# A cross-attention block with a routed feed-forward layer: ScalarE issues the transfer of the maxima rows

## The chip, the core and the metric

The kernel runs on one core of a Trainium2 chip. The metric is the device time of one execution in microseconds. Five engines run their own programs in order and meet only at semaphores: PE (TensorE), DVE (VectorE), ACT (ScalarE), POOL (GpSimd) and SP (SyncE, which here only issues transfers). Transfers run on 16 DMA engines, whoever issues them.

## What is computed

The input is 32 batches of 128 tokens of width 128, with a context of the same shape. Cut to what matters:

```
q, k, v = layernorm(x) @ Wq + bq, ctx @ Wk + bk, ctx @ Wv + bv        # 16 heads of width 8
s   = q k^T / sqrt(8)                                                  # 128 x 128 per head and batch
x1  = x + tanh(g0) * (softmax(s) v) @ Wout + ...
y   = layernorm(x1);  expert = argmax(y @ Wg)                          # 8 experts, 512 places each
out = x1 + tanh(g1) * gate * (relu(y @ W1[e] + b1[e]) @ W2[e] + b2[e])
```

A softmax needs the largest score of each row subtracted before the exponential. This kernel subtracts it inside a second matrix product: the negated maximum, split into two bf16 parts, stands in two more rows of the packed q operand, against rows of ones in the packed k operand.

## The kernel before, in words

**Tiles and stages.** The 32 batches are worked in 8 groups of four. A schedule of steps numbered `c` runs through all engines; step `c` belongs to group `g = c // 4` at place `j = c % 4`, and each engine does in step `c` the work of several batches at different ages: scores of batch `c` (`scores`, L476, in four quarters q of four heads), maxima of batch `c` on DVE (`top`, L735), the transposition of the maxima of batch `c-1` on PE (L537) and their eviction to `mrow` on ACT (L649), the shifted scores of batch `c-2` (`shifted`, L491, four quarters) and their exponentials on ACT (`exps`, L624), the products with the values of batch `c-3` (L505), and normalisation and output projection of batches `c-4` and `c-5`. The steps 8 to 23 run in a hardware loop; the others are written out.

**Packing.** q and k are kept as three bf16 parts each, and the matrix products run over the stacked parts. `pack` (L327) moves the parts of a whole group from `parts_k` and `parts_q` into `kp` and `qp`: six transfers of 128 KB for k and six for q. SP issues those of group g+1 in step `j == 2` of group g. It first waits until shifted scores of two groups back have been read (`p_T`, from group 2 on) and for `k_split`, later for `q_split`, which POOL (L258) or, at the start, DVE signals. Group g+1 can start its scores (L476) when all twelve have landed.

**The rows of maxima.** The 8 KB of `mrow` go into rows 48 and 49 of `qp` by one transfer a batch (L342), issued by SP in step `n+1` after it has waited for ACT's eviction (`a_m`). In step `j == 2` it stands between the six transfers of k and the six of q. PE waits for it (`m_in`) before the first quarter of the shifted scores of that batch, in step `n+2`.

**What orders the work.** SP's program is in order: whatever stands behind a wait for `a_m` is issued after it. In each step ACT evicts `mrow` between the exponentials of quarter 0 and those of quarter 1, and `shifted` uses two PSUM banks in turn, so that its quarter q waits for the exponentials of quarter q-2 (`a_exp`). After step 39 come eight experts of the feed-forward layer, which the change does not touch.

Of the kernel before, what the change touches and what calls it, by code (L numbers as in the profile page):

```python
# [27 lines left out]
GB = 4  # L28
# [7 lines left out]
def flamingo_kernel(nc, x, ctx_in, g_xattn, g_ffn, w_qkv, b_qkv, w_out, b_out, wg, w1, b1, w2, b2, consts, out):  # L36
    B, L, D = x.shape
# [10 lines left out]
    KR = SLOTS * HD  # L48
    KM = KR + 2
# [7 lines left out]
    with ExitStack() as ctx:  # L57
        def sb(name, shape, dt=F32):
            return ctx.enter_context(nc.sbuf_tensor(name, shape, dt))
# [4 lines left out]
        def sem(name):  # L64
            return ctx.enter_context(nc.semaphore(name))

        def sem2(name):
            return [sem(name + "0"), sem(name + "1")]
# [47 lines left out]
        qp = [sb(f"qp{i}", [P, HEADS, GT], BF16) for i in range(2)]  # L116
# [6 lines left out]
        mrow = [sb(f"mrow{i}", [2 * HEADS, P], BF16) for i in range(2)]  # L123
# [46 lines left out]
        c_in, q_in, k_in, m_in = sem2("c_in"), sem2("q_in"), sem2("k_in"), sem2("m_in")  # L170
# [7 lines left out]
        a_cT, a_xT, a_q, a_k, a_m = sem("a_cT"), sem("a_xT"), sem("a_q"), sem("a_k"), sem("a_m")  # L178
# [23 lines left out]
        def per_batch(v, r, per=1):  # L202

            return v if r is None else r * (per * BODY) + v

        def per_group(v, r, per=1):
            return v if r is None else r * (per * BODY // GB) + v

        def is_batch(n):
            return 0 <= n < B  # L210

        def is_group(g):
            return 0 <= g < NG
# [60 lines left out]
        def _(sp):  # L274
# [13 lines left out]
            def load_w1(e, at):  # L288

                sp.dma_start(w1s[e % 2][:], moved(w1[e % 2], at)).then_inc(w1_in[e % 2], 16)  # L290
# [6 lines left out]
            def ready(*values):  # L297

                for v in values:
                    if not isinstance(v, int):  # L300
                        sp.reg_mov(scratch, v)
# [27 lines left out]
            def step(c, r):  # L329
                j, g = c % GB, c // GB  # L330
                if j == 2 and is_group(g + 1):
                    pack(g + 1, r, 0, SLOTS)
                loads, stores = j == 0 and is_group(g + 2), j == 0 and is_group(g - 2)
                if j == 0:
                    ready(per_batch(c, r), per_group(g + 1, r), per_batch(GB * (g - 2) + GB, r))
                if is_batch(c - 1):
                    sp.wait_ge(a_m, per_batch(c, r))
                if is_batch(c - 1):
                    n, p = c - 1, (c - 1) % 2
                    G = n // GB  # L340
                    t0 = (n % GB) * L
                    sp.dma_start(qp[G % 2][KR:KM, :, t0:t0 + L], mrow[p][:]).then_inc(m_in[p], 16)  # L342
                if stores:
                    sp.wait_ge(v_x1, per_batch(GB * (g - 2) + GB, r))
                    sl = bass.ds(per_group((g - 2) * GB, r, GB), GB)
                    sp.dma_start(out_v[:, sl, :], rec[g % 2][:, :, D:2 * D]).then_inc(x1_out, 16)
                if loads:
                    if g + 2 >= 2:
                        sp.wait_ge(p_cT, per_group(g + 1, r))
                    sp.dma_start(c_sb[g % 2][:], ctx_v[:, bass.ds(per_group((g + 2) * GB, r, GB), GB), :]).then_inc(c_in[g % 2], 16)  # L350
                if j == 2 and is_group(g + 1):
                    pack(g + 1, r, SLOTS, 2 * SLOTS)
                if c == -8:
                    late_loads()
                if c == -7:
                    sp.dma_start(x_sb[:, 2 * GB:, :], x_v[:, 2 * GB:, :]).then_inc(x_in[2], 16)
                if c == -1:
                    sp.wait_ge(v_ones, 1)
                    for i in range(2):
                        sp.dma_start(kp[i][KR:KM, :, :], ones_row[:]).then_inc(s_ones, 16)  # L360
                if c == B + 2:
                    for e in range(2):
                        load_w1(e, None)
                        load_w2(e, None)
                    sp.dma_start(b1_all[:], b1.rearrange("e (f p) -> p e f", p=P),
                                 allow_slow_non_contiguous=True).then_inc(b12_in, 16)
                    sp.dma_start(b2_all[:], b2.rearrange("(a e) n -> a (e n)", a=1).broadcast_to([P, E * D])).then_inc(b12_in, 16)

            run_steps(step, sp)

            def load_xe(e, at):
# [45 lines left out]
        def _(pe):  # L417
# [48 lines left out]
            def scores(n, q, r):  # L466

                G, t0 = n // GB, (n % GB) * L
                if q == 0 and n % GB == 0:
                    pe.wait_ge(q_in[G % 2], per_group(96 * (G // 2) + 96, r, 48))  # L470
                    pe.wait_ge(k_in[G % 2], per_group(96 * (G // 2) + 96, r, 48))
                if 4 * n + q >= 2:
                    pe.wait_ge(v_red, per_batch(4 * n + q - 1, r, 4))
                for h in range(4 * q, 4 * q + 4):
                    o = (h % 4) * L
                    mm = nc.tensor.matmul(S[:, q % 2, o:o + L], qp[G % 2][0:KR, h, t0:t0 + L],  # L476
                                          kp[G % 2][0:KR, h, t0:t0 + L], start=True, stop=True)
                mm.then_inc(p_S, 1)
# [123 lines left out]
        def _(act):  # L602
# [23 lines left out]
            def step(c, r):  # L626
                j, g = c % GB, c // GB
                if is_batch(c - 4):
                    n = c - 4
                    act.wait_ge(p_O, per_batch(n + 1, r))  # L630
                    if n >= 2:
                        act.wait_ge(p_back, per_batch(n - 1, r))
                    nc.scalar.activation(oraw[n % 2][:], O[:, n % 2, :], ACT.Copy).then_inc(a_O, 1)
                if is_batch(c - 2):
                    exps(c - 2, 0, r)
                if j == 2 and is_group(g + 2):
                    H = g + 2
                    act.wait_ge(p_cT, per_group(H + 1, r))
                    if H >= 2:
                        act.wait_ge(p_v, per_group(H - 1, r))  # L640
                    nc.scalar.activation(cT[H % 2][:], X[:, 1, :], ACT.Copy).then_inc(a_cT, 1)
                if j == (3 if g + 2 else 2) and is_group(g + 2):
                    proj(1, g + 2, r)
                if is_batch(c - 1):
                    n = c - 1
                    act.wait_ge(p_m, per_batch(n + 1, r))
                    if n >= 2:
                        act.wait_ge(m_in[n % 2], per_batch(16 * (n // 2), r, 8))
                    nc.scalar.activation(mrow[n % 2][:], X[:, 0, 0:P // 2].bitcast(BF16)[0:2 * HEADS, :],  # L649
                                         ACT.Copy).then_inc(a_m, 1)  # L650
                if is_batch(c - 2):
                    exps(c - 2, 1, r)
                if j == (3 if g + 2 else 2) and is_group(g + 2):
                    first_part(1, g + 2, r)
                if is_batch(c - 2):
                    exps(c - 2, 2, r)
                if j == 2 and is_group(g + 2):
                    H = g + 2
                    act.wait_ge(p_xT, per_group(H + 1, r))
                    if H >= 1:  # L660
                        act.wait_ge(p_q, per_group(H, r))
                    nc.scalar.activation(xnT[:], X[:, 0, :], ACT.Copy).then_inc(a_xT, 1)
                if j == 3 and is_group(g + 2):
                    proj(0, g + 2, r)
                if is_batch(c - 2):
                    exps(c - 2, 3, r)
                if j == 1 and is_group(g - 2):
                    G = g - 2
                    act.wait_ge(p_nT, per_group(G + 1, r))
                    nc.scalar.activation(xn2T[:], X[:, 0, :], ACT.Copy).then_inc(a_nT, 1)  # L670
                if is_batch(c - 4):
                    n = c - 4
                    act.wait_ge(p_oT, per_batch(n + 1, r))
                    if n >= 2:
                        act.wait_ge(p_at, per_batch(n - 1, r))
                    nc.scalar.activation(onT[n % 2][:], X[:, 1, 0:L], ACT.Copy).then_inc(a_oT, 1)  # L676
                if j == 3 and is_group(g + 2):
                    first_part(0, g + 2, r)
                if j == 2 and is_group(g - 2):
                    G = g - 2  # L680
                    act.wait_ge(v_ldif, per_group(G + 1, r))
                    nc.scalar.activation(lexp[:], ldif[:], ACT.Exp).then_inc(a_lexp, 1)
# [448 lines left out]
```

## Time and profile before

| | |
|---|---|
| time, median of 3 runs | 491.91 us (491.57 to 496.6) |
| span of the profiled execution | 506.3 us |
| mean granted TensorE clock in it | 0.639 of full speed |
| PE busy | 393.1 us (78%) |
| ACT busy | 157.3 us (31%) |
| DVE busy | 233.6 us (46%) |
| POOL busy | 173.4 us (34%) |
| packets of the hardware queue q1, share of 16 engines | 31.4% |

The page gives no other time for the profiled execution than its span, which is 14.4 us above the median of the runs. The attention stage takes the first 400 us of the span. In the rows below, "L327" is a line of the kernel before, SPq, POOLq and ACTq are the instructions with which an engine issues transfers, and `[1.42 <-DMA qp<-mrow]` means that the engine was idle for 1.42 us before the instruction until that transfer landed.

### The profile page before, as it was taken

Reading aid. Unit: us, or ns where it says so; the run is one execution under the profiler, and the core shown is the slowest. Engines: PE = TensorE matmul, PEld = TensorE weight load, DVE = VectorE, ACT = ScalarE, POOL = GpSimd, SP = SyncE. Lnnn points to the kernel's source line nnn. Section 1 sums busy time; section 2 is a strip of 40 time slices with the busy share of each in tenths; the row PEclk is TensorE's granted clock in tenths of the full one; section 3 lists DMA queues with packets and bytes.
Section 4 is the critical chain, followed back from the end, with each engine's and each line's share of the span. In section 5 each row is a group of like instructions: output and inputs, shape, how many; then the busy total and the mean of one; then the engine's idle time right before and its main releaser. Section 6 shows DMA issues by size and latency. Waiting matters only on the chain.

```text
span 506.3 us, 8841 instructions
## 1 busy us (share of the span) xinstructions
PE 393.1 (78%) x3024; PEld 257.7 (51%) x3024; DVE 233.6 (46%) x710; ACT 157.3 (31%) x322; POOL 173.4 (34%) x200
## 2 busy tenths in 40 slices
PE   2437399999987959998796998479999525999950
PEld 0215256646654745665474565347665322676650
DVE  3609235726734863673586257245441311425440
ACT  1221143433433533333353345123333101313200
POOL 4535131322406522540642281041032260155463
PEclk9975555555557765555776559555555555999995
DMA  6863640521253254225315513530016014356320
GB/s 171 214 137 74 150 78 22 116 55 43 37 63 72 56 62 55 84 35 61 71 51 61 57 65 44 63 64 23 3 38 152 21 54 110 97 157 195 95 75 20
DMA packets 47748, 39.22 MB, mean 77 GB/s; under 512 B 8774, under 2 KB 43291, under 8 KB 47716
## 3 DMA queue, kind: packets, MB, share of 16 engines
q1 hardware_dynamic: 44004, 28.73, 31.4%
q0 software_dynamic: 3712, 10.07, 5.9%
q8 instruction: 19, 0.31, 0.3%
q14 instruction: 13, 0.11, 0.1%
HBM read 13.72 MB, written 12.65 MB: 52 GB/s over the span
## 4 chain that ended last, share of the span: by engine, by line
PE 54%; DMA 23%; SPq 7%; issue 4%; DVE 4%; POOL 3%; another core or an unknown queue 2%; ACT 1%; POOLq 0%; DVEq 0%; ACTq 0%
DMA qp<-parts_q 15%; PE O L505 9%; PE S L476 9%; PE TS L491 8%; SPq L327 6%; DMA qp<-mrow 5%; PE X L532 5%; PE X L578 4%; PE X L442 3%; PE X L527 3%; PE TS L568 2%; PE O L568 2%; PE X L436 2%; PE X L542 1%
## 5 line engine op out<-in xcount | busy, mean ns | idle before, releaser
L735 DVE TENSOR_REDUCE negm<-S 128x4 f32<-128x512 f32 x128 | 87.6, 688 | 87.3 <-PE S L476 85.1
L624 ACT ACTIVATE prob<-TS 128x512 f32<-128x512 f32 x128 | 75.5, 591 | 101.4 <-PE TS L491 100.9
L491 PE MATMUL TS<-qp,kp 50*128 50x128 bf16 x512 | 74.6, 293 | 28.1 <-DMA qp<-mrow 28.1
L476 PE MATMUL S<-kp,qp 48*128 48x128 bf16 x512 | 72.4, 289 | 21.8 <-DMA qp<-parts_q 19.2
L505 PE MATMUL O<-prob,vals 128*32 128x128 f32 x1024 | 79.7, 396 | 0.0
L476 PEld LDWEIGHTS S<-kp,qp 48*128 48x128 bf16 x512 | 41.1, 121 | 65.8 <-issue 40.2
L491 PEld LDWEIGHTS TS<-qp,kp 50*128 50x128 bf16 x512 | 53.2, 136 | 33.2 <-DMA qp<-mrow 29.7
L255 POOL TENSOR_TENSOR rest_k<-full_k,parts_k 128x512 f32<-128x512 f32 x7 | 8.1, 1155 | 107.5 <-ACT parts_k L617 107.5
L649 ACT ACTIVATE mrow<-X 32x128 bf16<-32x128 bf16 x32 | 8.5, 267 | 102.8 <-PE X L537 96.8
L505 PEld LDWEIGHTS O<-prob,vals 128*32 128x32 f32 x1024 | 25.9, 135 | 22.3 <-issue 17.4
L1013 POOL TENSOR_TENSOR fence_p<-pool_c 128x1 f32<-128x1 f32 x16 | 3.1, 192 | 98.8 <-DVE slot L883 61.4
L1040 POOL DMA_INDIRECT rec_dram<-rec,slot x32 | 31.9, 996 | 11.4 <-issue 11.4
L1094 POOL DMA_INDIRECT out_dram<-fin,tok x32 | 31.4, 980 | 12.3 <-issue 12.3
L1018 POOL TENSOR_TENSOR rs<-mv,pool_c 128x4 f32<-128x4 f32 x16 | 3.3, 204 | 93.1 <-DVE mv L799 61.6
L771 DVE TENSOR_TENSOR rec<-X,x_sb 128x128 f32<-128x128 f32 x32 | 9.2, 288 | 50.4 <-PE X L527 44.5
L532 PE MATMUL X<-cst,oraw 128*128 128x128 f32 x128 | 32.0, 397 | 0.1
L578 PE MATMUL X<-w2s,qp 128*128 128x128 f32 x256 | 29.7, 275 | 0.0
L578 PEld LDWEIGHTS X<-w2s,qp 128*128 128x128 f32 x256 | 29.2, 192 | 0.5 <-issue 0.5
L532 PEld LDWEIGHTS X<-cst,oraw 128*128 128x128 f32 x128 | 20.6, 198 | 6.0 <-issue 5.2
L809 DVE TENSOR_SCALAR xn<-x_sb,mv,rs 128x128 f32<-128x128 f32 (+1 forms) x32 | 21.5, 719 | 2.9 <-POOL rs L1020 2.9
L527 PE MATMUL X<-wout_g,onT 128*128 128x128 f32 x64 | 21.8, 442 | 1.0 <-ACT onT L676 0.9
L703 ACT ACTIVATE qp<-TS,b_act 128x512 f32<-128x512 f32 x16 | 10.9, 687 | 36.7 <-PE TS L568 25.9
(111 smaller groups left out, 566.4 us busy)
## 6 DMA issues: line engine op xcount, KB each, us to landing
kp<-parts_k SPq DMA_DIRECT2D x48, 128.0 KB
qp<-parts_q SPq DMA_DIRECT2D x48, 128.0 KB
rec_dram<-zeros POOLq DMA_DIRECT2D x8, 516.0 KB
xr<-rec_dram SPq DMA_DIRECT2D x8, 260.0 KB
c_sb<-in_ctx_dram SPq DMA_DIRECT2D x8, 256.0 KB, 3.0
out_dram<-rec SPq DMA_DIRECT2D x8, 256.0 KB, 2.4
w1s<-in_L_ffn_W_dram SPq DMA_DIRECT2D x8, 256.0 KB
w2s<-in_L_ffn_W_dram SPq DMA_DIRECT2D x8, 256.0 KB, 2.7
```

The lines of the kernel that those rows point to most:

```text
L327: sp.dma_start(dst, src).then_inc((k_in if side == "k" else q_in)[p], 16)
L476: mm = nc.tensor.matmul(S[:, q % 2, o:o + L], qp[G % 2][0:KR, h, t0:t0 + L], kp[G % 2][0:KR, h, t0:t0 + L], start=True, stop=True)
L491: mm = nc.tensor.matmul(TS[:, q % 2, o:o + L], kp[G % 2][0:KM, h, t0:t0 + L], qp[G % 2][0:KM, h, t0:t0 + L], start=True, stop=True)
L505: mm = nc.tensor.matmul(O[i * HV:(i + 1) * HV, n % 2, q * L:(q + 1) * L], vals[G % 2][:, k, h, :], prob[n % 2][:, h * L:(h + 1) * L], star ...
L527: nc.tensor.matmul(X[:, 0, 0:D], onT[(c - 5) % 2][:], wout_g[:], start=True, stop=True).then_inc(p_at, 1)
L532: mm = nc.tensor.transpose(X[:, 1, i * L:(i + 1) * L], oraw[c % 2][:, i * L:(i + 1) * L], ident)
L578: mm = nc.tensor.matmul(X[:, e % 2, t * P:(t + 1) * P], hid[e % 2][:, f, t * P:(t + 1) * P], w2s[e % 2][:, f, :], start=(f == 0), stop=(f ...
L624: nc.scalar.activation(prob[n % 2][:, q * 512:(q + 1) * 512], TS[:, q % 2, :], ACT.Exp).then_inc(a_exp, 1)
L735: V.tensor_reduce(negm[n % 2][:, 4 * q:4 * q + 4], S[:, q % 2, :].rearrange("p (h k) -> p h k", h=4), AX.X, ALU.max, negate=True).then_inc ...
L809: mm = V.tensor_scalar(xn[:, k, :], row, mv1[:, k, 0:1], rs1[:, 1, k:k + 1], ALU.subtract, ALU.mult)
L1040: G_.indirect_dma_start(rec_dram, bass.IndirectOffsetOnAxis(slot[p][:, k:k + 1], 0), rec[p][:, k, :], None, bounds_check=T - 1, oob_is_err ...
L1094: G_.indirect_dma_start(out_rows, bass.IndirectOffsetOnAxis(tok[p][:, t:t + 1], 0), fin[p][:, t, :], None, bounds_check=T - 1, oob_is_err= ...
```

## The change

The wait for `a_m` and the transfer of `mrow` leave SP's program and stand in ACT's, directly behind the eviction that they wait for. SP's program keeps all else in its order; a register that only this wait used is no longer set. The transfer's shape, source, target and semaphore are the same.

```diff
                 if j == 0:
-                    ready(per_batch(c, r), per_group(g + 1, r), per_batch(GB * (g - 2) + GB, r))
-                if is_batch(c - 1):
-                    sp.wait_ge(a_m, per_batch(c, r))
-                if is_batch(c - 1):
-                    n, p = c - 1, (c - 1) % 2
-                    G = n // GB
-                    t0 = (n % GB) * L
-                    sp.dma_start(qp[G % 2][KR:KM, :, t0:t0 + L], mrow[p][:]).then_inc(m_in[p], 16)
+                    ready(per_group(g + 1, r), per_batch(GB * (g - 2) + GB, r))
...
                     nc.scalar.activation(mrow[n % 2][:], X[:, 0, 0:P // 2].bitcast(BF16)[0:2 * HEADS, :],
                                          ACT.Copy).then_inc(a_m, 1)
+                    G, t0 = n // GB, (n % GB) * L
+                    act.wait_ge(a_m, per_batch(n + 1, r))
+                    act.dma_start(qp[G % 2][KR:KM, :, t0:t0 + L], mrow[n % 2][:]).then_inc(m_in[n % 2], 16)
                 if is_batch(c - 2):
                     exps(c - 2, 1, r)
```

In the order of SP's program, from the context load of step 0 to the context load of step 4. Before:

```order
L350 DMA c_sb<-in_ctx_dram 128x4x128 [waits p_cT]
L342 DMA qp<-mrow 2x16x128 [waits a_m]
L327 DMA kp<-parts_k 8x16x512 [waits a_k,k_split]
L327 DMA kp<-parts_k 8x16x512 x5
L342 DMA qp<-mrow 2x16x128 [waits a_m]
L327 DMA qp<-parts_q 8x16x512 [waits a_q,q_split]
L327 DMA qp<-parts_q 8x16x512 x5
L342 DMA qp<-mrow 2x16x128 [waits a_m] x2
L350 DMA c_sb<-in_ctx_dram 128x4x128 [waits p_cT]
```

Now (L343 is the context load's new line):

```order
L343 DMA c_sb<-in_ctx_dram 128x4x128 [waits p_cT]
L327 DMA kp<-parts_k 8x16x512 [waits a_k,k_split]
L327 DMA kp<-parts_k 8x16x512 x5
L327 DMA qp<-parts_q 8x16x512 [waits a_q,q_split]
L327 DMA qp<-parts_q 8x16x512 x5
L343 DMA c_sb<-in_ctx_dram 128x4x128 [waits p_cT]
```

The pack of group 1 has no wait for an eviction of ACT ahead of it or inside it any more. On ACT, the same stretch (steps 1 and 2) now reads as follows; L642 is the eviction, L646 the transfer and L617 the exponentials:

```order
L642 ACTIVATE mrow<-X 32x128 [waits p_m]
L646 DMA qp<-mrow 2x16x128 [waits a_m]
L617 ACTIVATE prob<-TS 128x512 [waits p_T]
L634 ACTIVATE cT<-X 128x512 [waits p_v,p_cT]
L642 ACTIVATE mrow<-X 32x128 [waits p_m]
L646 DMA qp<-mrow 2x16x128 [waits a_m]
L617 ACTIVATE prob<-TS 128x512 [waits p_T] x2
```

Each of the 32 evictions is followed by the wait and the transfer, ahead of the exponentials of the next quarter.

## Rows read from the trace of the kernel before

**Rows 1.** Waits of SP's queue (line, waited for: us in total, times, longest).
```profile
SPq L342 <- ACT mrow L649: 218.5, 27, 14.1
```

**Rows 2.** Waits of all engines, same columns: PE's two waits for these transfers.
```profile
PE TS L491 <- DMA qp<-mrow: 28.1, 8, 8.3
...
PE S L476 <- DMA qp<-parts_q: 19.2, 5, 7.7
```

**Rows 3.** Timeline of SP: start us, us, engine, line, operation, out<-in, count.
```profile
28.55 0.42 SPq L350 DMA_DIRECT2D c_sb<-in_ctx_dram  x1
43.07 0.63 SPq L342 DMA_DIRECT2D qp<-mrow  x1
...
88.99 4.27 SPq L327 DMA_DIRECT2D kp<-parts_k  x6
...
220.38 3.97 SPq L327 DMA_DIRECT2D kp<-parts_k  x6
227.77 0.67 SPq L342 DMA_DIRECT2D qp<-mrow  x1
228.54 3.92 SPq L327 DMA_DIRECT2D qp<-parts_q  x6
...
263.76 3.98 SPq L327 DMA_DIRECT2D kp<-parts_k  x6
```

**Rows 4.** Timeline of POOL: ends of the splits of group 1.
```profile
31.22 1.15 POOL L258 TENSOR_TENSOR parts_k<-rest_k,parts_k 128x512 bf16<-128x512 f32 x1
...
48.12 1.23 POOL L258 TENSOR_TENSOR parts_q<-rest_q,parts_q 128x512 bf16<-128x512 f32 x1
```

**Rows 5.** Timeline of PE, attention stage: waits in brackets.
```profile
45.11 0.58 PE L491 MATMUL TS<-qp,kp 50*128 50x128 bf16 x4 [0.20 <-DMA qp<-mrow]
...
61.22 0.60 PE L491 MATMUL TS<-qp,kp 50*128 50x128 bf16 x4 [6.92 <-DMA qp<-mrow]
...
72.05 0.60 PE L476 MATMUL S<-kp,qp 48*128 48x128 bf16 x4 [0.93 <-DMA qp<-parts_q]
...
102.13 0.60 PE L491 MATMUL TS<-qp,kp 50*128 50x128 bf16 x4 [1.42 <-DMA qp<-mrow]
...
113.84 0.60 PE L476 MATMUL S<-kp,qp 48*128 48x128 bf16 x4
...
236.09 0.61 PE L491 MATMUL TS<-qp,kp 50*128 50x128 bf16 x4 [1.64 <-DMA qp<-mrow]
...
248.33 0.60 PE L476 MATMUL S<-kp,qp 48*128 48x128 bf16 x4 [3.45 <-DMA qp<-parts_q]
...
279.46 0.61 PE L491 MATMUL TS<-qp,kp 50*128 50x128 bf16 x4 [4.00 <-DMA qp<-mrow]
...
291.57 0.60 PE L476 MATMUL S<-kp,qp 48*128 48x128 bf16 x4
```

**Rows 6.** POOL's own transfers of zeros: size; issue ns least/median/most.
```profile
rec_dram<-zeros POOLq DMA_DIRECT2D x8, 516.0 KB
...
L1071 POOL DMA_DIRECT2D rec_dram<-zeros x8: 712/732/938, 11.5 to 88.2; - x8
```

**Rows 7.** Timeline, one step at half clock and one at full clock.
```profile
253.06 0.27 ACT L649 ACTIVATE mrow<-X 32x128 bf16<-32x128 bf16 x1 [3.06 <-PE X L537]
253.23 0.57 ACT L624 ACTIVATE prob<-TS 128x512 f32<-128x512 f32 x1
...
255.20 0.63 PE L491 MATMUL TS<-qp,kp 50*128 50x128 bf16 x4
...
305.97 1.19 ACT L624 ACTIVATE prob<-TS 128x512 f32<-128x512 f32 x2
...
307.05 0.39 PE L491 MATMUL TS<-qp,kp 50*128 50x128 bf16 x4
```

**Rows 8.** Windows: us, busy PE PEld DVE ACT POOL, PEclk, DMA share, GB/s.
```profile
45.00:61.00 16.00, 6.37 (x41) 4.61 (x41) 8.88 (x13) 3.73 (x7) 6.92 (x8) 0.50 0.70 158
...
263.00:269.00 6.00, 4.84 (x72) 3.48 (x64) 5.80 (x10) 3.27 (x7) 5.84 (x6) 1.00 0.37 51
```

## The prediction

> **What bounds the kernel now.** I read the waits of SP's queue first. SP stands 218.5 us before `mrow` transfers, waiting for ACT's evictions [rows 1]. That is no cost in itself, since SP computes nothing, but its program is in order, so each wait also holds back what is queued behind it. The waits of the engines show where this reaches PE, the busiest engine: PE stands 28.1 us in 8 waits for an `mrow` transfer and 19.2 us in 5 waits for packed q [rows 2]. Together 47 us, and these are the only transfers of the attention stage that hold PE in its middle.
>
> The timelines of SP and PE say how they come about. In group 5's pack SP issues six transfers of k at 220.38, `mrow` at 227.77 and six of q at 228.54 [rows 3]. `mrow` is 8 KB, but PE gets it only at 236.09, 8.3 us after its issue [rows 5]. With nothing ahead of it the same transfer takes 2.04 us from issue to PE's use (43.07 to 45.11) [rows 3, 5]. So it waits its turn behind k in SP's queue. The packed q then releases PE at 248.33, 27.95 us after the pack began; in the next group the pack starts at 263.76 and PE starts the scores at 291.57, 27.81 us later, this time without a wait in front of them [rows 3, 5]. These two numbers are nearly the same though PE stood 1.64 us for `mrow` in one and 4.00 us in the other. From group 3 on, a group's start is thus the start of its pack plus about 27.9 us, and PE's wait for `mrow` lies inside this time. The start of the pack itself hangs on PE (shifted scores of the second step), 15.4 us after the group's start (248.33 to 263.76) [rows 3, 5].
>
> Group 1 is different. Its k parts are ready when POOL ends at 31.22 + 1.15 = 32.37 [rows 4]. SP had finished its last issue at 28.97, but stands until 43.07 for the first `mrow`, and only then issues k [rows 3]. Its q parts are ready at 48.12 + 1.23 = 49.35 [rows 4]. k and q, and some of POOL's eight transfers of zeros, of 516 KB each [rows 6], then meet in one stretch: 158 GB/s from 45 to 61 us, DMA share 0.70 [rows 8]. PE waits 6.92 us for the second `mrow` and 0.93 us for q, and starts group 1 at 72.05 [rows 5].
>
> **The change, part by part.**
>
> *Group 1.* With the first `mrow` out of its way, SP issues k at 32.4 instead of 43.8, 11.4 us earlier, while PE and DVE still wait for the first scores. q cannot come earlier than 49.4. Most of k has then landed before q starts. Behind 49.4 lie 0.79 MB of q and, at most, three times 0.52 MB of zeros [rows 6]: 2.3 MB, at the 158 GB/s of this stretch [rows 8] 14.7 us, with about 2 us from issue to use as above: q at 66. PE's own arrival is 72.05 - 0.93 - 6.92 = 64.2, as long as the first `mrow`, issued near 43.1, does not stand behind k. So group 1 starts at about 66, against 72.05: **-6.0 us**. Bounds: with q there earlier, PE's arrival decides, so -7.9; if all six transfers of k stand before the first `mrow`, and take the 15.7 us that lie between 220.38 and 236.09, it lands at 48.1 instead of 45.1 [rows 3, 5], PE arrives 3.0 us later, at 67.2, so -4.9, and if k is slowed as much again, -1.9.
>
> *Group 2.* Its pack begins at 88.99, 16.9 us after the group's start, and has landed before PE starts the scores at 113.84, since no wait stands there [rows 3, 5]. This pack took at most 24.85 us. What PE loses between is the wait of 1.42 us for `mrow` [rows 5]. It goes: **-1.4 us**. Bounds: 0, if this pack takes 27.9 us like the later ones, where it even costs 1.7 (88.99 + 27.9 = 116.9 against 113.84 - 1.42 = 112.4, in all 3.0 us later than before), and -1.4.
>
> *Groups 3 to 7.* Of the 28.1 us, 0.20, 6.92 and 1.42 are spent by now; the other five waits hold 19.6 us. They disappear at `mrow`, and what is late next is packed q: the pack still starts 15.4 us after the group and still needs its 27.9 us. SP issues q about 4 us earlier, directly behind k, but k occupies the transfers until 236 in the example and q was already queued at 228.5, so nothing moves. **0 us**, and PE's wait for q grows by about 19.6 us from 19.2, less what group 1 saves. Bounds: 0 and -1.4 a group, the latter if the packs are as quick as group 2's; that is a rival.
>
> *Interleaving.* One `mrow` a group, that of the last step, went behind q and now goes beside it. 8 KB against the pack's 1.57 MB is 0.5%, 0.14 us of 27.9; the nearest thing measured for a small transfer is the 2.04 us above, nearly all latency. I take 0.2 us for each of the five groups: **+1.0 us**, bounds 0 and 4.
>
> *ACT.* 32 issues. SP's take 0.67 us, POOL's issues of zeros 0.73 us [rows 3, 6]; ACT's own are not in the trace. I take 0.7 us, 22 us in all on an engine that is 31% busy. Before, the exponentials of quarter 1 started at 253.23, 0.17 us after the eviction; now they start behind eviction and issue, at 253.33 + 0.7 = 254.0, and end by 254.6. Fourth-quarter shifted scores, which need their bank, start at 255.20 [rows 7]: hidden with 0.6 us to spare. In a step at full clock the same exponentials (305.97, 0.6 us each) end at 306.57, and the quarter that waits starts at 307.05 [rows 7]; there 0.8 us of delay leave 0.3 us on PE. The clock is full in few stretches, one of them 263 to 269 [rows 8]. Over some four such steps that decide a pack's start: **+1.0 us**. Lower bound 0; the upper one is the slower rival.
>
> *SP.* 32 issues of 0.66 us fewer. SP never bounds but in group 1, which is counted. Context loads and stores of x1 also come earlier or at the same time; none is waited for in the middle of the stage.
>
> Sum: -6.0 - 1.4 + 0 + 1.0 + 1.0 = **-5.4 us**. The profiled execution spans 506.3 us and would span 500.9. The median of the runs is 14.4 us below that span, and I know no row that says where; I take the same difference off it: 491.91 - 5.4 = 486.5.
>
> **A rule against the change.** With nothing ahead of it in SP's queue `mrow` takes 2.04 us, behind k 8.3 us [rows 3, 5]; whether ACT's queue lets it pass k no row of this trace shows. The Trainium skill says in "DMA: Bandwidth & Descriptors", section "Issuing engines are not separate DMA queues", that transfers from several issuing engines run on the same engines and interleave, and that another issuer saves only the time of the issue. The same page, in "Queues, rings and completion order", has an engine take turns between the queues. By the first the waits for `mrow` would stay; by the second they would go.
>
> **Rivals.**
>
> 1. *`mrow` still waits behind k.* PE's later waits for `mrow` stay, group 2 gives nothing, and the first `mrow` may stand behind the early k: group 1 gives between -1.9 and -6.0, ACT costs 1 us, so 487 to 491, and with -4.9 it is 488. The 19.6 us of groups 3 to 7 change nothing, being hidden either way. For it: 8 KB took 8.3 us behind k. Chance 0.22. The page's first rule comes out here.
>
> 2. *Packs are quicker without the profiler.* The runs are 14 us shorter than the profiled span. If the later packs take 24.85 us or less there, PE is not waiting for q in groups 3 to 7, and an `mrow` wait of about 1.4 us each goes for good: five more times 1.4, 7 us more, 479.5; if these waits are as long as in the trace up to 472, but then the packs are slow too. Against it: nothing shows where the 14 us are. Chance 0.18.
>
> 3. *ACT becomes the bound, slower than before.* If an issue on ACT holds it for P us, the exponentials end at 253.33 + P + 0.6, and PE's fourth quarter at 255.20 waits once P is over 1.27 us [rows 7]. About 24 steps are not under a wait for q. To be slower by 1% the loss must be 4.9 + 7.4 = 12.3 us, 0.5 us a step, so P must be over 1.8 us; at P = 2 it is 0.73 x 24 = 17.5 us, so 491.9 - 7.4 + 17.5 = 502. The rows nearest to it, 0.67 and 0.73 us, speak against it [rows 3, 6]. Chance 0.09.
>
> 4. *The clock falls otherwise.* From start to pack, group 5 takes 15.4 us and group 1 takes 16.9 us with the same work [rows 3, 5]; a stretch at full clock, 263 to 269, begins about where group 5's pack does [rows 8]. With PE's waits moved from `mrow` to q the full stretches will lie elsewhere: if three of them miss the part that decides, 3 times 1.5 to 2 us are lost, 486.5 + 5 = 491.5, no change. Chance 0.13.
>
> **How the numbers follow.** The forecast, 486.5 us, has 0.38. A measurement of this kernel tells about 1%, 4.9 us, from no change; the border of faster is 487.0. Of the forecast's chance 0.23 lies below it and 0.15 above; rival 2 lies below (0.18), rival 1 mostly above (0.04 below, 0.18 above), rival 4 above (0.02 below, 0.11 above). Slower is rival 3 and 0.01 of rival 4. That gives faster 0.47, same 0.43, slower 0.10. The range from 478 to 493 leaves out rival 3 and the far end of rival 2. The likeliest case alone would be 484 to 489.
>
> **What would show it.** Right: group 1's k issued near 32.4 and its first scores near 66; no wait of PE for `mrow` over 1 us, and the total for q near 30 us or more; from group 3 on still 27.9 us from the pack's first issue to the scores; the exponentials of quarter 1 about 0.8 us later behind the eviction. Wrong: waits for `mrow` still near 20 us (rival 1), 25 us or less from pack to scores in the later groups (rival 2), PE waiting for the exponentials (rival 3), or a pack's start over 17 us after its group's in most groups (rival 4).

## The result, and the profile after

The changed kernel takes **511.02 us** (median of 4, 510.2 to 520.18), the kernel before 494.25 us in the same comparison. The ratio is **1.036**, 95% interval 1.028 to 1.043: 3.6% slower. Forecast were 486.5 us, with 478 to 493 as the range and 0.10 for slower. The change is not a gain that was missed but a loss of some 18 us.

The two traces hide part of this: their spans are 508.4 us after and 506.3 us before. Executions of one kernel lie up to 15 us and more apart here, and the trace of before shows a long one. The traces are therefore compared by the lengths inside a group. From group 3 on these repeat to within some 2 us in the kernel before.

The waits of the engines after, same columns as [rows 2]:

```profile
PE TS L484 <- DMA qp<-mrow: 52.0, 9, 9.2
...
PE S L469 <- DMA qp<-parts_q: 12.6, 3, 9.1
```

PE's waits for the maxima were to vanish from 28.1 us; they are 52.0. Its waits for packed q fell from 19.2 to 12.6. The largest shares of the chain that ended last are now the following; before, packed q stood there with 15% and the maxima with 5%.

```profile
DMA qp<-mrow 15%; PE O L498 9%; PE S L469 8%; PE TS L484 8%; DMA qp<-parts_q 6%; PE X L525 5%; PE X L571 5%; PE TS L561 3%; PE X L435 3%; PE X L520 3%; PE O L561 3%; PE X L429 3%; SPq L327 2%; PE X L432 2%; DVE negm L731 2%
```

SP's timeline after, the answer to [rows 3]:

```profile
32.36 7.64 SPq L327 DMA_DIRECT2D kp<-parts_k  x6
...
117.35 3.97 SPq L327 DMA_DIRECT2D kp<-parts_k  x6
121.42 5.57 SPq L327 DMA_DIRECT2D qp<-parts_q  x6
...
166.39 3.94 SPq L327 DMA_DIRECT2D kp<-parts_k  x6
170.44 5.44 SPq L327 DMA_DIRECT2D qp<-parts_q  x6
...
216.74 3.98 SPq L327 DMA_DIRECT2D kp<-parts_k  x6
```

ACT's issues of the maxima in these packs, and PE where it waits for them (timeline, the answer to [rows 5]):

```profile
122.45 0.62 ACTq L646 DMA_DIRECT2D qp<-mrow  x1
...
173.78 0.62 ACTq L646 DMA_DIRECT2D qp<-mrow  x1
```

```profile
64.45 0.40 PE L469 MATMUL S<-kp,qp 48*128 48x128 bf16 x4 [1.28 <-DMA qp<-parts_q]
...
136.65 0.61 PE L484 MATMUL TS<-qp,kp 50*128 50x128 bf16 x4 [8.86 <-DMA qp<-mrow]
...
188.30 0.61 PE L484 MATMUL TS<-qp,kp 50*128 50x128 bf16 x4 [7.83 <-DMA qp<-mrow]
```

The reader is to see the order. Packed q is issued at 170.44, directly behind k; the maxima follow at 173.78. They reach PE at 188.30, **21.9 us** after the pack's first issue, against 15.7 before (220.38 to 236.09, [rows 3, 5]). The next pack starts at 216.74, 28.4 us later. In the group before it the maxima are issued 5.1 us after the first k, with fewer transfers of q ahead, and PE has them after 19.3 us (117.35 to 136.65). From pack to pack these two groups take 49.0 and 50.4 us, and the two that follow 47.8 and 47.6; before, the time from group 5's pack to the next is 263.76 - 220.38 = 43.4 us [rows 3].

The maxima's transfers are on a queue of their own, q10, beside SP's q1 (packets, MB, share of 16 engines):

```profile
q1 hardware_dynamic: 42916, 28.47, 30.4%
q10 hardware_dynamic: 1088, 0.26, 0.4%
```

### The profile page after: what moved, and what is told of

Its sections match the earlier page's. It is cut to its first block, busy times and chain, and to the rows that moved or that the text cites. A ratio compares the mean times of both kernels' runs of the same rounds, so it can differ in the third digit from the quotient of the medians.

```text
span 508.4 us, 8827 instructions
## 1 busy us (share of the span) xinstructions
PE 381.6 (75%) x3024; PEld 248.8 (49%) x3024; DVE 232.8 (46%) x710; ACT 157.1 (31%) x322; POOL 173.4 (34%) x200
## 4 chain that ended last, share of the span: by engine, by line
PE 57%; DMA 23%; issue 5%; DVE 5%; POOL 3%; SPq 3%; ACT 1%; POOLq 0%; ACTq 0%; DVEq 0%
DMA qp<-mrow 15%; PE O L498 9%; PE S L469 8%; PE TS L484 8%; DMA qp<-parts_q 6%; PE X L525 5%; PE X L571 5%; PE TS L561 3%; PE X L435 3%; PE X L520 3%; PE O L561 3%; PE X L429 3%; SPq L327 2%; PE X L432 2%; DVE negm L731 2%
## 5 line engine op out<-in xcount | busy, mean ns | idle before, releaser
L484 PE MATMUL TS<-qp,kp 50*128 50x128 bf16 x512 | 72.0, 285 | 53.8 <-DMA qp<-mrow 52.0
L617 ACT ACTIVATE prob<-TS 128x512 f32<-128x512 f32 x128 | 73.9, 597 | 119.0 <-PE TS L484 104.5
L469 PE MATMUL S<-kp,qp 48*128 48x128 bf16 x512 | 69.9, 281 | 14.9 <-DMA qp<-parts_q 12.6
L484 PEld LDWEIGHTS TS<-qp,kp 50*128 50x128 bf16 x512 | 50.7, 131 | 60.0 <-DMA qp<-mrow 53.0
L498 PE MATMUL O<-prob,vals 128*32 128x128 f32 x1024 | 77.1, 385 | 0.0
L469 PEld LDWEIGHTS S<-kp,qp 48*128 48x128 bf16 x512 | 39.6, 118 | 56.9 <-issue 32.6
L642 ACT ACTIVATE mrow<-X 32x128 bf16<-32x128 bf16 x32 | 8.5, 266 | 97.3 <-PE X L530 97.3
L1090 POOL DMA_INDIRECT out_dram<-fin,tok x32 | 31.3, 978 | 11.8 <-issue 11.8
L525 PE MATMUL X<-cst,oraw 128*128 128x128 f32 x128 | 30.8, 385 | 0.1
L571 PE MATMUL X<-w2s,qp 128*128 128x128 f32 x256 | 29.7, 275 | 0.0
```

Of the source, the lines that this page charges most:

```text
L484: mm = nc.tensor.matmul(TS[:, q % 2, o:o + L], kp[G % 2][0:KM, h, t0:t0 + L], qp[G % 2][0:KM, h, t0:t0 + L], start=True, stop=True)
L498: mm = nc.tensor.matmul(O[i * HV:(i + 1) * HV, n % 2, q * L:(q + 1) * L], vals[G % 2][:, k, h, :], prob[n % 2][:, h * L:(h + 1) * L], star ...
L525: mm = nc.tensor.transpose(X[:, 1, i * L:(i + 1) * L], oraw[c % 2][:, i * L:(i + 1) * L], ident)
L571: mm = nc.tensor.matmul(X[:, e % 2, t * P:(t + 1) * P], hid[e % 2][:, f, t * P:(t + 1) * P], w2s[e % 2][:, f, :], start=(f == 0), stop=(f ...
L617: nc.scalar.activation(prob[n % 2][:, q * 512:(q + 1) * 512], TS[:, q % 2, :], ACT.Exp).then_inc(a_exp, 1)
L1090: G_.indirect_dma_start(out_rows, bass.IndirectOffsetOnAxis(tok[p][:, t:t + 1], 0), fin[p][:, t, :], None, bounds_check=T - 1, oob_is_err= ...
```

## The experiments

Theory 1 (order): a transfer waits for what was issued ahead of it, on whichever of the two queues; the change put q ahead of the maxima. Theory 2: ACT's queue is served late beside SP's. Theory 3: ACT's issue delays its exponentials.

**e0_before.** No edit.

> The kernel before, unchanged, for a second trace. The shown trace of before spans 506.3 us while the median of its runs is 494; the changed kernel's runs are 511 with a trace of 508.4. If the shown trace is of an execution in which the TensorE clock was low (0.639), this one should span about 490 with a granted clock near 0.7 and the same 27.9 us from a pack's first issue to the next group's scores. If instead the packs are quicker without disturbance, it shows 25 us or less there.

Times 506.34 and 494.58 us; the trace spans 504.5 us at a clock of 0.640. The expectation of a short span failed, as did the guess about the clock: 0.640 against 0.639 in the first trace. The 27.9 us held (group 3's pack, issued at 134.81, to the scores at 162.63, is 27.8). The packs aren't where the long executions lose. The start varies: group 0 began at 43.13 here, at 36.60 in the first trace of before, which is 1.8 us longer, so the start alone doesn't explain a long execution. In the other traces it began at 36 to 44 us (in e9, whose first pack is cut in two, at 31.5).

**e1_q_held.** The changed kernel, and in SP's step:

```diff
                 if j == 2 and is_group(g + 1):
+                    if is_batch(c - 1):
+                        sp.wait_ge(a_m, per_batch(c, r))
                     pack(g + 1, r, SLOTS, 2 * SLOTS)
```

> The changed kernel, with one wait given back to SP: before it issues the six transfers of packed q it waits for the eviction of the maxima (a_m), as before; the maxima still go by ACT. Theory 1 (order): the change made SP issue q right behind k, so that the maxima, issued 1 to 5 us later, now stand behind k and part of q and share the rest; with the wait back PE's 52 us of waits for them fall to 30 or less and the time to 486 to 494 us. Theory 2 (ACT's queue is served late or slowly beside SP's whatever the order): waits and time stay near 52 and 511. Theory 3 (the issue on ACT holds up the exponentials): the time stays near 511.

516.46 us, ratio to before 1.025 (1.017 to 1.032); before itself had a median of 503.84 us in this comparison, so the time isn't to be set beside the 511.02 above. It is not the 486 to 494 of theory 1, and yet the waits came down as theory 1 says:

```profile
PE TS L486 <- DMA qp<-mrow: 29.3, 10, 5.2
```

The timelines tell why (SP, ACT, PE):

```profile
172.07 3.94 SPq L327 DMA_DIRECT2D kp<-parts_k  x6
179.46 3.90 SPq L327 DMA_DIRECT2D qp<-parts_q  x6
```
```profile
179.46 0.62 ACTq L648 DMA_DIRECT2D qp<-mrow  x1
```
```profile
189.94 0.61 PE L486 MATMUL TS<-qp,kp 50*128 50x128 bf16 x4 [3.79 <-DMA qp<-mrow]
```

SP and ACT wait for the same semaphore and issue at the same instant, 179.46. PE has the maxima 17.87 us after the first k, 2.2 us later than before. By the packet records in the trace the transfers of a pack follow each other every 2.2 us, and the first packet of the maxima comes 15.2 us after the first k instead of 13.1: one transfer of q got ahead. The granted clock was low in this trace (0.597). The run doesn't separate the theories; the next two do.

**e5_q_behind_issue.** The changed kernel; SP's q waits for something that stands behind ACT's issue:

```diff
                 if j == 2 and is_group(g + 1):
+                    if is_batch(c - 2):
+                        sp.wait_ge(a_exp, per_batch(4 * (c - 2) + 2, r, 4))
                     pack(g + 1, r, SLOTS, 2 * SLOTS)
```

> The changed kernel, in which SP's six transfers of q wait until ACT's exponentials of the second quarter are done; these stand behind ACT's issue of the maxima, so that q cannot slip ahead of it, as one transfer of q did in the previous experiment (the first packets of the maxima came 15.1 us after the pack's first issue instead of 13.0). Theory 1 (order of issue over both queues): packets at 13.0 us, PE served at 15.7 us, as in the kernel before, PE's waits for the maxima at 18 to 25 us in all, and with group 1's early k 485 to 492 us. Theory 2 (ACT's queue served late beside SP's): packets still 15 us or later and 505 us or more. Theory 3 (ACT's issue delays the exponentials): PE waits for exponentials and stays above 500.

```profile
172.14 3.94 SPq L327 DMA_DIRECT2D kp<-parts_k  x6
180.90 3.89 SPq L327 DMA_DIRECT2D qp<-parts_q  x6
```
```profile
179.53 0.62 ACTq L648 DMA_DIRECT2D qp<-mrow  x1
```
```profile
187.87 0.60 PE L486 MATMUL TS<-qp,kp 50*128 50x128 bf16 x4 [1.66 <-DMA qp<-mrow]
```

The maxima still go by ACT's queue and now reach PE 15.73 us after the first k, before's value; the next pack starts at 216.02, 43.9 us after this one. That refutes theory 2. The total, 504.51 us, is not the 485 to 492 that theory 1 was to give: ratio 1.020 (1.006 to 1.035), so by the totals some half of the 3.6% is still there, within a wide interval. PE's waits were 32.6 us, not 18 to 25. Theory 3 named a time above 500 us, which came, and waits of PE for the exponentials, which did not: they are 1.8 us in this trace. Groups 3 to 6 have their old length, so what is left of the loss stands outside them; where, stays open.

**e6_sp_one_q_first.** The kernel before, with the early k of e3 below and one q ahead of the maxima, ACT not involved:

```diff
+                if j == 2 and is_group(g + 1):
+                    pack(g + 1, r, SLOTS, SLOTS + 1)
+                # the wait for a_m and the transfer of mrow stand here in this step
+                if j == 2 and is_group(g + 1):
+                    pack(g + 1, r, SLOTS + 1, 2 * SLOTS)
```

> The kernel before with the early k of group 1, all on SP, and one of the six transfers of q issued ahead of the maxima of the packing step. This is the order that the changed kernel has at best, without ACT. Theory 1: packets of the maxima 15.1 us after the pack's first issue, PE served at 17.8, each of the later groups some 2 us longer than before: 10 us more than the same kernel with the maxima ahead of q, 497 to 510 us. Theories 2 and 3, which need ACT: as the kernel with early k, 487 to 492.

```profile
169.79 3.98 SPq L327 DMA_DIRECT2D kp<-parts_k  x6
173.87 0.61 SPq L327 DMA_DIRECT2D qp<-parts_q  x1
177.19 0.67 SPq L359 DMA_DIRECT2D qp<-mrow  x1
177.90 3.26 SPq L327 DMA_DIRECT2D qp<-parts_q  x5
```
```profile
187.68 0.60 PE L500 MATMUL TS<-qp,kp 50*128 50x128 bf16 x4 [3.81 <-DMA qp<-mrow]
```

17.89 us from the first k to PE, against 17.87 in e1: the same order gives the same delay with or without ACT. The next pack comes at 217.42, 47.6 us after this one, in both. The time, 502.54 us (4 runs, 492.72 to 511.82), lies in the range of 497 to 510, but is too scattered for a ratio. The separation of the theories rests on the delay and the length of the groups.

**e2_sp_q_first.** The kernel before; in step `j == 2` the wait and the transfer of `mrow` stand behind all six of q:

```diff
-                if is_batch(c - 1):
+                if is_batch(c - 1) and j != 2:
                     sp.wait_ge(a_m, per_batch(c, r))
...
                     pack(g + 1, r, SLOTS, 2 * SLOTS)
+                if is_batch(c - 1) and j == 2:
+                    # the same wait and transfer
```

> The kernel before, all on SP, with the transfer of the maxima of the packing step moved behind the six transfers of q instead of ahead of them. Theory 1 (order): the maxima now wait for all twelve transfers, some 28 us from the first issue instead of 15.7, PE waits 12 us or more in each of seven groups and the time rises by 50 to 85 us, to 545 to 580. Theory 2 and theory 3, which blame ACT's queue or ACT's issue, expect the time of the kernel before, 490 to 497.

586.0 us, ratio 1.153 (1.144 to 1.161), even above the 545 to 580 that theory 1 gave. Timelines of SP and PE:

```profile
262.58 3.96 SPq L327 DMA_DIRECT2D kp<-parts_k  x6
266.65 5.38 SPq L327 DMA_DIRECT2D qp<-parts_q  x6
272.14 2.05 SPq L359 DMA_DIRECT2D qp<-mrow  x1
```
```profile
290.86 0.60 PE L498 MATMUL TS<-qp,kp 50*128 50x128 bf16 x4 [14.19 <-DMA qp<-mrow]
```

28.3 us from the first k to PE. The order alone, all on SP, costs over four times what the change cost (15.3% against 3.6%). This is theory 1 in its full form.

**e3_k1_early and e10_k1_early_again.** The kernel before; the first half of `pack` for group 1 in step 1, ahead of the first maxima:

```diff
-                if j == 2 and is_group(g + 1):
+                if c == 1 or j == 2 and c != 2 and is_group(g + 1):
                     pack(g + 1, r, 0, SLOTS)
```

> The kernel before, with the six transfers of k of group 1 issued one step earlier, ahead of the wait for the first maxima instead of behind it: the part of the change that the forecast counted at -6.0 us, alone. If that term is right: k issued near 32.4, group 1's scores 6 us earlier and 485 to 489 us in all. If the later groups swallow it: 492 to 495.

> The kernel before with the early k of group 1 alone, once more, since too few undisturbed executions were there for a ratio: 1.2% faster than before, 484 to 490 beside 490 to 494. If the later groups swallow the start, the same as before.

The trace of e3 spans 487.4 us, and group 1 starts 67.08 - 38.13 = 28.95 us after group 0, against 72.05 - 36.60 = 35.45 before:

```profile
38.13 1.03 PE L476 MATMUL S<-kp,qp 48*128 48x128 bf16 x8 [9.04 <-DMA qp<-parts_q]
...
67.08 0.58 PE L476 MATMUL S<-kp,qp 48*128 48x128 bf16 x4 [3.75 <-DMA qp<-parts_q]
```

That is 6.5 us at its place, as forecast (6.0). In the total it is hardly to be seen: e10's ratio is 0.998 (0.990 to 1.006), while the medians over all executions are 0.6% (e3) and 1.9% (e10) below before's. The forecast of 1.2% is not confirmed, and a gain of up to 1% is not excluded. Group 0 itself begins up to 8 us apart from trace to trace, as much as the edit moves.

**e7_two_k_behind.** With the early k, and from group 2 on two of the six k behind the maxima:

```diff
-                    pack(g + 1, r, 0, SLOTS)
+                    pack(g + 1, r, 0, SLOTS if c == 1 else 4)
                 # wait for a_m and transfer of mrow, as before
                 if j == 2 and is_group(g + 1):
+                    if c != 2:
+                        pack(g + 1, r, 4, SLOTS)
                     pack(g + 1, r, SLOTS, 2 * SLOTS)
```

> The kernel before with the early k of group 1, and with two of the six transfers of k issued behind the maxima from group 2 on. The maxima now have four transfers ahead of them instead of six: packets near 10 us after the pack's first issue, PE served by 12 to 13 us. If the landing of q, 27.9 us after the first issue, bounds a group as closely as the maxima do (as the forecast said), PE's waits move to q and the time stays at 485 to 492; if the maxima alone bound it, each group is 3 us shorter and the time 470 to 480.

495.3 us, ratio 0.991 (0.988 to 0.994), under 1% from before, and above the 485 to 492 expected. PE's waits:

```profile
PE S L478 <- DMA qp<-parts_q: 31.3, 8, 9.4
PE TS L493 <- DMA qp<-mrow: 1.4, 3, 0.8
```

The waits for the maxima are gone (1.4 us), and those for q are 31.3 us instead of 19.2. A pack still follows the last after 43.4 us (216.06 to 259.48; 43.4 to 45.4 over the stage). The 470 to 480 of the maxima as the only bound didn't come. So the landing of q does bound a group as closely as the maxima did.

**e8_after.** The changed kernel, unchanged.

> The changed kernel again, unchanged, beside the others on one chip: 508 to 513 us if undisturbed, with PE served with the maxima 19 to 22 us after a pack's first issue in groups 2 to 6. All theories expect the same.

531.37 us (its quickest execution 510.29), too scattered for a ratio. The trace is of an execution of 538 us. SP, ACT and PE:

```profile
134.78 3.96 SPq L327 DMA_DIRECT2D kp<-parts_k  x6
...
186.51 3.94 SPq L327 DMA_DIRECT2D kp<-parts_k  x6
190.56 5.29 SPq L327 DMA_DIRECT2D qp<-parts_q  x6
...
340.06 3.89 SPq L327 DMA_DIRECT2D kp<-parts_k  x6
```
```profile
193.91 0.62 ACTq L646 DMA_DIRECT2D qp<-mrow  x1
```
```profile
208.44 0.60 PE L484 MATMUL TS<-qp,kp 50*128 50x128 bf16 x4 [7.84 <-DMA qp<-mrow]
```

PE has the maxima 21.9 us after the first k, as in the longest group of the trace above, and the next pack starts at 238.18, 29.7 us later. Here all of groups 3 to 6 are of this kind, and take 50.2 to 51.7 us.

**e9_halves.** The kernel before with the early k, and each pack cut by columns into halves of two batches (the main lines of the edit):

```diff
+                    cols = slice(half * GT // 2, (half + 1) * GT // 2)
+                    dst = (kp if side == "k" else qp)[p][s * HD:(s + 1) * HD, :, cols]
...
+                if j == 3 and is_group(g + 1) and c != -1:
+                    pack(g + 1, r, 0, 2 * SLOTS, 1)
...
+                if q == 0 and n % GB == 2:
+                    pe.wait_ge(q_in2[G % 2], per_group(96 * (G // 2) + 96, r, 48))
+                    pe.wait_ge(k_in2[G % 2], per_group(96 * (G // 2) + 96, r, 48))
```

> The kernel before with the early k of group 1, all on SP, and each pack cut by columns into the halves of two batches: step j == 2 issues k's first half (6 x 64 KB), the maxima, q's first half; step j == 3 issues the maxima and then both second halves, which batches 2 and 3 wait for. If a group is bound, as the experiments so far say, both by the maxima behind six transfers of k (15.7 us) and by the landing of all q (27.9 us), both bounds fall here: maxima near 10 us, q's first half near 15 us after the first issue; PE's waits of 40 us nearly vanish, a group takes the 40 us of PE's own work at half clock instead of 45.5, and the time is 455 to 475. If packets of 512 B cost as much each as packets of 1 KB, the pack takes twice as long and the time is above 500.

**477.39 us**, ratio to before 0.968 (0.955 to 0.980), the fastest of all, though above the 455 to 475 expected. (By the medians of all its and before's executions it is 477.39 against 503.28.) Its waits:

```profile
PE TS L500 <- DMA qp<-mrow: 19.1, 7, 6.3
...
PE S L485 <- DMA qp<-parts_q: 5.6, 2, 3.3
```

Together 24.7 us against 47.3 before. Groups 3 and 4 still take 44.5 and 44.1 us from pack to pack, with hardly a wait; groups 5 and 6 take 40.7 and 41.3. Windows over groups 4 and 5 say why (columns as in [rows 8]):

```profile
163.62:207.74 44.12, 43.81 (x335) 28.76 (x336) 25.28 (x78) 17.53 (x36) 16.83 (x19) 0.50 0.36 61
207.74:248.47 40.73, 34.32 (x335) 23.42 (x336) 24.36 (x78) 17.14 (x36) 15.50 (x18) 0.71 0.40 65
```

PE's own work for one group is 43.8 us where the granted clock was 0.50, not the 40 of the expectation; before, with its waits, PE was busy 38.3 of the 43.4 us from 220.38 to 263.76, at a mean of 0.62. So at half clock PE's work is as long as a whole group before, and that is the next limit. The other outcome named, packets of 512 B as dear as those of 1 KB, didn't come: in group 4's first halves their mean is 59 ns, against 141 ns for one of 1 KB before.

For the length of groups over the whole stage, three more rows of SP's timeline before, and the one of after that answers to the last:

```profile
131.51 3.97 SPq L327 DMA_DIRECT2D kp<-parts_k  x6
174.84 3.98 SPq L327 DMA_DIRECT2D kp<-parts_k  x6
...
307.46 3.96 SPq L327 DMA_DIRECT2D kp<-parts_k  x6
```
```profile
312.06 3.89 SPq L327 DMA_DIRECT2D kp<-parts_k  x6
```

Groups 4 and 5 before took 220.38 - 174.84 = 45.5 us and 263.76 - 220.38 = 43.4 us [rows 3]. Side by side, in us, for the groups from group 3's pack to group 7's (the last column is the sum of the two ahead of it):

| kernel | ahead of the maxima | first k to PE's use | from there to the next pack | pack to pack |
|---|---|---|---|---|
| before (SP issues) | 6 k | 15.6 to 15.7 | 27.7 to 29.8 | 43.3 to 45.5 |
| e5 (ACT issues) | 6 k | 15.6 to 16.0 | 28.2 to 29.9 | 43.9 to 45.5 |
| e1 (ACT issues) | 6 k, 1 q | 17.7 to 17.9 | 27.8 to 29.7 | 45.5 to 47.7 |
| e6 (SP issues) | 6 k, 1 q | 17.8 to 17.9 | 29.7 | 47.6 |
| after (ACT issues) | 6 k, 2 to 5 q issued | 19.2 to 21.9 | 28.3 to 29.7 | 47.6 to 50.4 |
| after again, e8 | 6 k, 5 q issued | 21.9 to 22.0 | 28.3 to 29.7 | 50.2 to 51.7 |
| e2 (SP issues) | 6 k, 6 q | 28.1 to 28.3 | 29.7 | 57.9 to 58.0 |

The third column follows the order of issue, whoever issues. The fourth hardly moves. It is 29.7 us where the record has the clock at 0.50 throughout (e6, 187.68 to 217.42) and 27.7 where its mean is 0.68 (before, 236.09 to 263.76).

## Why the prediction was wrong

- **The step that failed** is "Groups 3 to 7: 0 us". It says that SP issues q about 4 us earlier, directly behind k, "so nothing moves". Nothing moves for q; but q now stands ahead of the maxima, which before stood ahead of q because SP's wait for `a_m` held q back. I priced the removed wait by what stood behind it and not by what it had kept behind the maxima. Measured: PE served 19.2 to 21.9 us after the first k instead of 15.7. The sign named for being right, 27.9 us from the pack's first issue to the next scores, failed with it:

```profile
248.10 0.60 PE L469 MATMUL S<-kp,qp 48*128 48x128 bf16 x4
```

That is 31.4 us after 216.74, and without a wait for q, whose last packet had landed 26.8 us after the first issue, as before.
- **The bound was half read.** PE's use of the maxima comes 15.7 us into the pack and the next group's scores 12.1 us later (279.46 to 291.57, [rows 5]): 27.8 us. That is the length of the way over q, 27.9. I took the agreement of 27.95 and 27.81 as a sign that only q counts; it was two ways of one length. Which of them ends last goes with the granted clock between the two points (windows before, columns as in [rows 8]):

```profile
236.09:248.33 12.24, 8.79 (x86) 5.10 (x87) 5.07 (x17) 5.48 (x11) 4.61 (x5) 0.78 0.49 54
279.46:291.57 12.11, 12.11 (x86) 6.71 (x87) 4.07 (x17) 4.76 (x10) 3.42 (x3) 0.50 0.49 54
```

In the first PE needs 8.79 us at 0.78 and then waits for q; in the second the same work fills all 12.11 us at 0.50, and q is there already. e7 shows that q does bound it, e1, e2 and e6 that the maxima do too. What was added to the maxima came out in the group, since the rest of it kept its length: 2.2 more in e6 for 47.6 us, against 43.3 to 45.5, 6.2 more in e8 for 51.7 (238.18 - 186.51), 12.6 more in e2 for 58.0.
- **The sum of it.** Between the packs of group 3 and group 7, four groups, after takes 312.06 - 117.35 = 194.7 us and before 307.46 - 131.51 = 176.0, by SP's issues in the two traces: 18.8 us more. Up to group 3's pack, after had been 14.2 us ahead (131.51 - 117.35). In e8, the same kernel, that lead isn't there: its pack starts at 134.78, and the four groups take 340.06 - 134.78 = 205.3 us. The nearest thing to a like comparison is e3's trace, of a quick execution of before (span 487.4) that has the early k too:

```profile
118.89 3.97 SPq L327 DMA_DIRECT2D kp<-parts_k  x6
...
296.54 3.96 SPq L327 DMA_DIRECT2D kp<-parts_k  x6
```

After's span is 21.0 us longer: 1.5 less up to group 3's pack, 194.7 - 177.7 = 17.1 more over the four groups, 5.5 more behind group 7's pack. The four groups thus hold the larger part of a loss of some 18 us. The 5.5 us are not explained, and e5, whose four groups take 177.5 us as e3's do, keeps 7.7 us ahead of group 3's pack and 5.5 behind group 7's: that the totals are the sum of the groups is not shown.
- **Rival 1** said that the maxima would still wait behind k. That was right, and it had the larger truth in it, but its price, 487 to 491, took for granted that they would wait no longer than before. The Trainium skill's sentence ("DMA: Bandwidth & Descriptors", section "Issuing engines are not separate DMA queues"), that another issuer saves only the time of the issue, fits better than the turns of "Queues, rings and completion order": e1 and e6 agree to 0.02 us. It isn't the whole of it either: in e8 the maxima were issued 3.4 us after the first q, when 5 q had been issued, and their first packet came 17.2 us after the first k, behind the six k and some 2 of these 5 q (21.9 us to PE's use, not 28.3). Why only 2, no run shows.
- **Rivals 2, 3 and 4.** ACT's issue takes 0.62 us, near the 0.7 taken, and PE's waits for the exponentials after come to 1.6 us (below): rival 3 forecast slower, but by the wrong mechanism. Packs are no quicker in other executions: e3's trace, of one that took 489.29 us, has 27.9 us again (118.89 to 146.74), which disposes of rival 2. Rival 4's sign, a pack over 17 us after its group's start in most groups, didn't come: after, it is 16.3 to 16.4 us in three of groups 3 to 6 (248.10 to 264.50, for one) and 17.7 in one. How much of the total the clock moves, no run shows.

PE's waits for the exponentials after (ACT itself stands 13.3 us in 18 such waits behind its eviction, 0.8 us at most):

```profile
PE TS L484 <- ACT prob L617: 1.6, 5, 0.4
```

- **Group 1** was right: k issued at 32.36 (forecast 32.4), scores at 64.45 (forecast 66).
- **Group 2** was not: PE's wait for the maxima, which was to vanish from 1.42 us, is 5.09 (at 97.62), for the same reason as in the later groups. The working of this term also slips: 116.9 against 113.84 is 3.0 us and not 1.7, and a bound of 0 doesn't cover it.
- **Interleaving**, held to be 0.2 us a group, is part of the failed step. It priced the maxima of a group's last step; those that came beside q are the packing step's. By the packet records their 32 packets take 2.7 us beside q after and 0.9 us before.

## What to carry to other kernels

A wait that is taken out of an in-order queue also frees what it had held back, and that may get ahead of a small urgent transfer; write down the order of issue over all queues before and after, and price each transfer by the bytes ahead of it. Where two ways to the same event are equally long, neither can be counted as hidden: cutting one gives nothing (e7), lengthening one costs in full (e6, e2). A small transfer that must come soon needs fewer bytes issued ahead of it, not another engine to issue it; cutting the bulk transfer by the order in which it is used, together with the early k, gave 3.2% (e9, 2.0 to 4.5%; the early k alone gave nothing clear).

## What the hardware showed that was not expected

- Two issuers, one order: with the same transfers ahead, the maxima took 17.89 us by SP's queue and 17.87 us by ACT's, 15.7 by either with q held.
- The record of the granted clock can be wrong for a whole stage, and the instructions tell. Two windows from PE's use of the maxima to the next pack, of e6 and of e2:

```profile
187.68:217.42 29.74, 29.74 (x230) 18.77 (x231) 15.18 (x51) 10.84 (x22) 13.00 (x15) 0.50 0.27 53
290.86:320.59 29.73, 29.73 (x230) 18.77 (x231) 14.88 (x51) 10.85 (x22) 13.01 (x15) 1.00 0.12 36
```

The same 230 matmuls take the same time, 29.7 us, at a recorded 0.50 and at a recorded 1.00; before, they took 24.2 us at 0.68 (236.09 to 263.76). So e2's mean of 0.987 is not the clock that its attention stage had, and neither is e8's 0.881, whose window from 208.44 to 238.18 shows 1.00 and 29.73 us as well. A clock from the record is worth holding against the length of the same instructions in another stretch.
- Packs ran at two speeds in all traces: twelve transfers in 15 to 19 us in group 2 and in 25 to 26 us from group 3 on, by the packet records (mean packet 91 and 141 ns before). The cause stays open.
